# A recommender network on one core: spreading the history groups evenly over the fp32 passes, and the order of the work inside the steps

## What is computed

```python
item_img_feat = gelu(ln(item_emb_d128 @ mm_w + mm_b))
target = item_table[item_id] + item_img_feat
seq_emb = item_table[item_seq]                       # (B, 50, 128)
x = concat([t, seq_emb, t - seq_emb, t * seq_emb])   # t: target, broadcast
scores = relu(x @ aw1 + ab1) @ aw2 + ab2             # masked where item_seq == 0
hist_feat = einsum('bs,bsd->bd', softmax(scores), seq_emb)
sparse = stack([like, view, item_id, item_img, hist])      # 5 fields
z = mean(sparse, -1)
se = sparse * sigmoid(relu(z @ se_w1 + se_b1) @ se_w2 + se_b2)
bil = [(se[i] @ bil_W[i]) * se[j] for i < j]               # 10 pairs
dnn_in = concat([se, bil])                                 # (B, 15 * 128)
xc = dnn_in
for i in range(2):
    xc = dnn_in * (xc @ cross_K[i] + cross_bias[i]) + xc
h = gelu(ln(xc @ w1 + b1)); h = gelu(ln(h @ w2 + b2))
return sigmoid(h @ w3 + b3)
```

## Time and profile before

| | |
|---|---|
| median of 3 runs | 2,060.68 us (2,059.72 to 2,065.24) |
| the profiled execution | 2,058.15 us |
| its span | 2,056.3 us, 34,832 instructions |
| busy: PE, PEld | 1,929.3 us (94%), 1,521.1 us (74%) |
| busy: DVE, ACT, POOL | 1,281.5 us (62%), 880.2 us (43%), 883.5 us (43%) |
| gathers (L524) | 800 of rows of `e`, 1,043 ns each |
| fp32 products (L682) from 100 to 500 us | 1,800 records, 231.5 us |
| DMA | 240.92 MB, 117 GB/s |

### The profile page before, as it was taken

The page is one execution under the profiler, slowest core; times in us unless marked ns, Lnnn a source line. Parts: engine busy times, 40 slices in busy tenths (PEclk is TensorE's granted clock), DMA queues, the critical chain, the costliest instruction groups (busy, mean ns, idle before and its releaser), DMA issues. The chain is left out here.

```text
span 2056.3 us, 34832 instructions
## 1 busy us (share of the span) xinstructions
PE 1929.3 (94%) x10808; PEld 1521.1 (74%) x10808; DVE 1281.5 (62%) x2216; ACT 880.2 (43%) x1942; POOL 883.5 (43%) x854
## 2 busy tenths in 40 slices
PE   4488999988999999999999999999999999999997
PEld 3276888766777786777777887777777888888885
DVE  5545455557777666677877665667877564445553
ACT  1523233435445346654544236654454343322234
POOL 7777767676767203755757003756630000000000
PEclk7699999998999999999999999999999999999998
DMA  8444445343444532333435532334433543333320
GB/s 242 125 115 116 135 128 144 109 134 89 125 117 137 198 92 77 111 115 111 136 101 154 185 98 72 115 110 114 130 91 100 172 134 106 91 98 100 98 63 1
DMA packets 108341, 240.92 MB, mean 117 GB/s; under 512 B 22640, under 2 KB 27776, under 8 KB 108032
## 3 DMA queue, kind: packets, MB, share of 16 engines
q1 hardware_dynamic: 72144, 157.57, 25.5%
q0 software_dynamic: 27136, 55.63, 10.5%
q10 hardware_dynamic: 8880, 25.50, 3.4%
HBM read 225.83 MB, written 12.79 MB: 116 GB/s over the span
## 5 line engine op out<-in xcount | busy, mean ns | idle before, releaser
L524 POOL DMA_INDIRECT e<-in_item_table,idx_all x800 | 834.5, 1043 | 613.4 <-POOLq L544 380.9
L1402 DVE TENSOR_TENSOR Wl<-raw,Wh 128x640 fp32r<-128x640 f32 (+1 forms) x366 | 295.6, 808 | 254.8 <-DVEq L1401 253.2
L1024 ACT ACTIVATE Wh<-raw 128x640 fp32r<-128x640 f32 (+1 forms) x366 | 261.8, 721 | 389.6 <-ACTq L1023 388.5
L704 PE MATMUL psum<-X1h,Wh 128*128 128x512 f32 x900 | 361.6, 402 | 5.9 <-PEq L702 5.3
L705 PE MATMUL psum<-X1l,Wh 128*128 128x512 f32 x900 | 352.6, 392 | 0.0
L706 PE MATMUL psum<-X1h,Wl 128*128 128x512 f32 x900 | 351.7, 391 | 0.0
L704 PE MATMUL psum<-X0h,Wh 128*128 128x512 f32 x675 | 272.2, 403 | 0.0
L705 PE MATMUL psum<-X0l,Wh 128*128 128x512 f32 x675 | 263.7, 391 | 0.0
L706 PE MATMUL psum<-X0h,Wl 128*128 128x512 f32 x675 | 263.6, 391 | 0.0
L993 ACT ACTIVATE e<-e,pw 128x128 f32<-128x128 f32 x800 | 242.8, 388 | 15.3 <-ACTq L200 15.3
L704 PEld LDWEIGHTS psum<-X1h,Wh 128*128 128x128 f32 x900 | 169.7, 189 | 47.6 <-issue 12.5
(11 more groups left out here) (169 smaller groups left out, 2530.6 us busy)
## 6 DMA issues: line engine op xcount, KB each, us to landing
raw<-in_cross_K SPq DMA_DIRECT2D x399, 320.0 KB
raw<-in_w SPq DMA_DIRECT2D x51, 256.0 KB
e<-in_item_table,idx_all POOLq DMA_INDIRECT x800, 2.5
dnn_scratch<-dn ACTq DMA_DIRECT2D x12, 960.0 KB
kept<-in_cross_K SPq DMA_DIRECT2D x24, 320.0 KB, 3.8
x1f<-dnn_scratch ACTq DMA_DIRECT2D x3, 2048.0 KB, 9.2
x1f<-dnn_scratch ACTq DMA_DIRECT2D x3, 1792.0 KB, 16.6
e<-in_w SPq DMA_DIRECT2D x9, 256.0 KB, 4.8
```

Source lines behind the costliest of these rows:

```text
L524: nc.gpsimd.indirect_dma_start(out=dst, out_offset=None, in_=table, in_offset=bass.IndirectOffsetOnAxis(ap=idx_all[:, t, s:s + 1], axis=0) ...
L704: m0 = mm(out, wh, Xh[:, 0:T, k, :], start=(k == 0), stop=False)
L1024: af(Wh[:, split_slot(w), 0:n], raw[:, rs, 0:n], ACT.Copy).then_inc(hi_done, 1)
L1402: v.tensor_tensor(Wl[:, rs, 0:n], raw[:, rs, 0:n], Wh[:, slot, 0:n].bitcast(F32), ALU.subtract).then_inc(lo_done, 1)
```

## The change

It does five things. `SPREAD` has other steps for tiles 2 to 5. In `make_plan` the last group of tiles 1 to 3 has its open, score and summed one step earlier. Share and neg of the tiles whose first group lies in the passes, or in step 60, come one step later. Inside the steps of the passes, TensorE makes the turn of the target and the turn of a tail between parts 1 and 2, and the turn of the scores behind part 2; ScalarE makes the high splits and the copy of the tail ahead of exps and weigh, the copy now in the lift's step, not in the pair's. In the opening VectorE does a history ahead of the maximum of a later group.

```diff
-SPREAD = ((0, 2, 4, 6, 8), (10, 13, 16, 19, 22), (25, 28, 31, 34, 37), (40, 42, 44, 46, 48), (50, 52, 54, 56, 58))
+SPREAD = ((0, 2, 4, 6, 8), (10, 12, 14, 17, 19), (22, 24, 27, 29, 32), (34, 36, 39, 41, 44), (46, 48, 51, 54, 56))
...
-                plan[k + 2].open = plan[k + 3].score = plan[k + 4].summed = (t, g)
-                plan[k + 4].mid = True
-                done = k + 4
+                lag = 1 if t < TILES[0] and g == NG - 1 else 2
+                plan[k + lag].open = plan[k + lag + 1].score = plan[k + lag + 2].summed = (t, g)
+                plan[k + lag + 2].mid = True
+                done = k + lag + 2
...
         elif s <= solo_end:
-            fetch, aim, swing, share, neg = s - 6, s - 4, s - 1, s, s + 1
+            fetch, aim, swing, share, neg = s - 6, s - 4, s - 1, s + 1, s + 2
...
                 solo_products(p.solo, p.n, 1)
+                if p.swing is not None:
+                    head_turn()
+                if p.lift is not None:
+                    tail_turn(p.lift)
+                solo_products(p.solo, p.n, 2)
                 if p.score:
                     score_turn(mscore)
-                if p.swing is not None:
-                    head_turn()
-                solo_products(p.solo, p.n, 2)
                 if p.share is not None:
                     head_share(p.share)
-                if p.lift is not None:
-                    tail_turn(p.lift)
...
             def solo_step(p):
                 c, k = p.chunk, p.k
-                if p.pair is not None:
-                    tail_copy(p.pair)
                 if p.fetch is not None:
                     head_fetch(p.fetch)
...
                     copy_tT(p.swing)
+                for n in p.split:
+                    x_hi(c, 0, n)
+                if p.lift is not None:
+                    tail_copy(p.lift)
                 if p.summed:
                     exps(*p.summed)
                     weigh(*p.summed)
                 if p.gate is not None:
                     tail_gate()
-                for n in p.split:
-                    x_hi(c, 0, n)
...
+                for q in p.sums:
+                    history(*q)
                 if p.open:
                     hidden_max(p.open[0], groups(p.open[0])[p.open[1]][1])
                 if p.pair is not None:
                     tail_pairs(p.pair)
-                for q in p.sums:
-                    history(*q)
```

## The result

The changed kernel takes 2,048.32 us (median of 5 runs, 2,043.79 to 2,050.55) where the kernel before takes 2,062.54 beside it (5 runs, 2,059.72 to 2,066.49): ratio 0.9926, 95% interval [0.991, 0.9941]. The direction was right, the size was not.

A forecast was written before the change was run, and what follows sets the result against it. TensorE alone (446 us) and POOL alone (446.9) were to end the passes; 2 added gave 449, a gain of 34.8. Step 60 added 3.0 and 1.9, less 3 and 2: gain 34.7, forecast 2,025 us, range 2,014 to 2,043.

The forecast's parts named there:

- the start: Opening, VectorE's history put ahead of a maximum that waits for the hidden product: between -3 and +1 us, taken as -2.
- Behind the passes: Step 60: 3.0 us shorter and 1.9 from full clock, against 3 for late x splits and 2 unseen.
- The tails: TensorE's waits around the tails of tiles 1 to 4: of 17.9 us some 6 stay.
- The bilinear product: Tile 1's tail: its 6.67 us wait goes with the earlier tail copy, and the 3.0 us before the pass's products too.
- The turn of the scores: Moved behind the third part in the passes: eleven waits, 9.2 us in sum, shrink to 2.
- The clock: TensorE's busy time in the passes: 331 us less 9 for the low clock, so 322 at full clock.
- Score rows: Waits late in the passes before score rows (7.0 us) and split products (5.3): about 4 of 12.3 stay.
- The even spread: Passes' table of steps: zero in sum for work, but VectorE's crowded end eases, leaving about 4 of 12.3 us of waits.
- POOL: Gathers in the passes no longer wait for histories; POOL alone would end the passes at 446.9 us.
- Waits move: Rival, 20%: VectorE's new order in the passes costs about 0.7 us at each of 20 groups plus low clock, 2,033 to 2,046.
- Slower: Rival, 3%: gathers at 15.0 us for ten instead of 13.1 use up the gain; at 16, 18 us slower, 2,076.

The follow-up runs named there:

- the later fold: Changed kernel with fold and gates of tiles 2 to 4 one step behind the last group's history, turn three, bilinear product later: 2,029.8 us, again 2,031.0.
- the cut: Changed kernel with tiles 2 to 4's fold and gates one step, turn of the fields two, bilinear product three steps behind the last group's stages: 2,032.9 us.

## Why the prediction was wrong

**Step by step.** I had the first split product at 449 us; it came at 474.0. Against the sum of TensorE's chain (108.8 + 325 + 12 + 2 = 447.8) the 26.2 us are: 0.6 late instead of 2.0 early at the start (2.6), busy 333.2 instead of 325 (8.2), idle 29.5 instead of 14 (15.5). Behind the passes the forecast was 2.1 us too cautious. The start says nothing on the opening's new order: two executions of one and the same kernel, the later fold, began the passes at 109.9 and 111.5.

- *The tails.* The step that failed is "of 17.9 us some 6 stay", with 3, 1, 0 and 2 before the turns. Measured: 4.89, 4.39, 3.07 and 2.25, 14.6. I counted when the history starts within its step, but not what VectorE carries over from the step before: tile 1's row starts 1.4 us later than my count (184.69, behind a history that began at 177.35), and tile 2's later still. So 8.6 of the 15.5 us of idle time that I had not counted stand before the turns. What the row costs the whole time is shown by the cut: 7.4 us beyond moving the turn, 15.4 with it, and 18.5 in the later fold, where the turn comes another step later and the pairs stand apart from score rows.
- *The bilinear product.* Right that 6.67 goes, and the reason stands: with old table and old lag the new orders leave 0.2 us of these waits in the passes. But with the new table and lag the wait stays away from tile 1 under ScalarE's old order too (under both old orders 4.15 us of it are back at tile 4), so in the changed kernel that order's 6.4 us come mostly by hidden products, splits and the turn of the scores. The 3.0 us of the pass's products were put down to the same copy wrongly: under the new orders they stay (2.96) with old table and old lag together, and with the new table and lag they are gone even under both engines' old orders.
- *The turn of the scores.* Forecast 2 us of waits, measured 0.2. As a term of the sum it was worth nothing: the rival run without it took as long, since the waits moved to the turns of the fields. I let each wait that went be time gained, as in "so most vanish wholly".
- *The clock.* I priced all busy time at full clock and said so ("322"). The waits that stay bring the low clock back. The five lows that the later fold does not have lose 5.2 x 0.50, 5.7 x 0.30, 5.2 x 0.33 twice and 5.0 x 0.34, some 9.4 us; the busy time differs by 7.8. Hence 325 was near for a kernel without these waits: the later fold has 325.4, tile 1's low included. It also fits that 12.6 us less idle time than in the kernel before came with 2.3 us more busy time, 3 of it the group that moved in: the waits taken away were in part short ones, behind which the clock had stayed at 1.00 (1.18 us at 280.33, 1.19 at 358.59), and those that came were long.
- *Score rows.* "I expect about 4 to stay", of 12.3 with the split products: 6.8 stay before the score rows and 5.2 before the split products. Two of 2.28 us come from the bank shared with the pairs, and 1.50 at 169.79 comes with the shorter lag of tile 1's last group, not with the moved turn of the scores: it stays when the turn is put back (1.51), and is in no version with the old lag.
- *The even spread.* It does what the step said only when VectorE's row is cut: worth 8 to 11 us then, and nothing, perhaps less, in the changed kernel.
- *POOL.* I had its last gather of tile 5 done at 427.1 and landed at 429.6. It was issued at 423.49, so with the 3.5 us of the earlier trace rows it landed at some 427.0, within 3 us. None of tile 5's gathers waits for rows any more; the 7.22 of the earlier trace rows is gone, and only the first of tile 6, below, and the eleventh wait, 2.10 and 1.54 us:

```profile
423.49 0.94 POOL L525 DMA_INDIRECT e<-in_item_table,idx_all  x1 [0.30 <-issue]
426.54 0.94 POOL L525 DMA_INDIRECT e<-in_item_table,idx_all  x1 [2.10 <-POOLq L545]
```

But I let it bind ("the two meet"), and no transposes are in the changed kernel's list of waits. It is near: the later fold, 18 us earlier, has two such waits, 0.5 us the longest.

**The rivals.** "Waits move" was the one that came, 20%, and its price of 20 us was about right (34.7 less 14 is 21), though not as it was told: not 0.7 us at each of twenty groups but 2 to 5 us at each of four tails. Its spells of the low clock were right. It reached to 2,046, and the range was cut at 2,043; the result lies above both. In *Slower*, going from 15.0 to 16 us for ten gathers is worth some 20 us over twenty groups, not 18.

## What to carry to other kernels

Before moving an instruction on the engine that waits, add up what stands in a row on the engine that it waits for, carried over from the step before, and see who else reads from behind that row: if the row is the cause, moving one reader hands part of the wait to the next (8 us gained here), and cutting the row as well ends it (15 us with both, 18.5 in the later fold). Waits must not be summed as gains: of many short ones, most may only be holding an engine back from a longer one behind. And parts of a change can have the other sign once another part is mended, so a part that brings nothing (the table here) is tried again behind the mend before it is thrown away.

## What was unexpected of the hardware

A wait of TensorE can cost close to twice its length: between the changed kernel and the later fold 9.0 us of idle time came with 7.8 us of slower matmuls. It is no fixed price. ScalarE's old order brought 4.8 us of idle time with 1.7 of busy, and the old turn of the scores, which trades long waits for short ones, 1.0 more of idle time with 4.9 less of busy. The length of the wait did not need to be great: behind 2.28 us at 269.35 and 2.25 us at 415.04 the clock was 0.70 and 0.66 for five to six microseconds. Yet in the later fold a wait of 2.17 us left the clock alone:

```profile
277.46 1.13 PE L669 MATMUL psum<-x0f,bil 128*128 128x128 f32 x8 [2.17 <-DVEq L1339]
```

```profile
277.40:283.00 5.60, 5.54 (x44) 1.00 0.52 153
```

The Trainium skill (TensorE: Matmul & The Clock Gate, Why this matters for your kernels) advises to leave no long idle gaps between bursts of matmuls, because the clock goes back to its lower level; the rows agree in kind (a clock of 0.50 behind the 4.39 us wait), and show it behind waits as short as 2.25 us. What part of it lies in the wait alone and what in the sparse work around it was not tried.
